# A linear-attention and expert kernel: VectorE makes attention's rows of batches 1 and 3 in front of a residual and of the router, and the scores' low half in front of w1's

## The reference

```python
x = x + attention(layernorm(x))      # q, k = elu(.)+1;  v
#   per row:  s += k v^T;  z += k;  out = (q s) / (q z + 1e-6);  out @ Wo + bo
x = x + moe(layernorm(x))
#   logits = x @ router_w^T;  two largest of 8, softmax over the two
#   y_e = gelu(x @ w1_e^T + b1_e) @ w2_e^T + b2_e;  sum of the two, weighted
```

## Time and profile before

| | us |
|---|---|
| median of 3 runs | 1016.1 (1013.57 to 1018.55) |
| profiled execution | 1024.98 |
| its span, first to last instruction | 1023.2 |

### The profile page before, as it was taken

The page is one execution under the profiler, slowest core; times in us unless marked ns, Lnnn a source line. Parts: engine busy times, 40 slices in busy tenths (PEclk is TensorE's granted clock), DMA queues, the critical chain, the costliest instruction groups (busy, mean ns, idle before and its releaser), DMA issues. The chain is left out here.

```text
span 1023.2 us, 33647 instructions
## 1 busy us (share of the span) xinstructions
PE 913.0 (89%) x10722; PEld 740.2 (72%) x10723; DVE 758.2 (74%) x2280; ACT 680.7 (67%) x1295; POOL 658.2 (64%) x580
## 2 busy tenths in 40 slices
PE   6788899899989998999987559899999999999994
PEld 3577677767766677766766338678999999999994
DVE  5788788888898888889887566456666666666673
ACT  7868888898888888898875414445555555555552
POOL 3245877788778877887773543347655665656565
PEclk9999899999999999999998779999999999999998
DMA  6726744554455354645451743435655556555554
GB/s 172 203 76 204 249 126 147 170 161 136 150 152 176 124 152 149 182 128 147 139 156 44 283 136 69 69 60 94 95 95 90 98 89 98 89 98 88 94 92 50
DMA packets 102583, 131.31 MB, mean 128 GB/s; under 512 B 15056, under 2 KB 89296, under 8 KB 101648
## 3 DMA queue, kind: packets, MB, share of 16 engines
q1 hardware_dynamic: 74336, 92.54, 32.4%
q0 software_dynamic: 25680, 35.01, 18.6%
q10 hardware_dynamic: 2464, 2.38, 0.7%
HBM read 64.29 MB, written 65.60 MB: 127 GB/s over the span
## 5 line engine op out<-in xcount | busy, mean ns | idle before, releaser
L1907 POOL DMA_INDIRECT out<-yt,to_token x135 | 216.6, 1604 | 176.2 <-DMA out<-yt,to_token 80.4
L1269 DVE SCALAR_TENSOR_TENSOR ahl<-pS,ahl 128x512 f16<-128x512 f32 x240 | 161.2, 682 | 42.1 <-ACT ahl L980 39.7
L980 ACT ACTIVATE ahl<-pS 128x512 f16<-128x512 f32 x240 | 142.2, 599 | 49.8 <-PE pS L652 36.0
L1783 POOL DMA_INDIRECT expert_in<-xn,cur x128 | 131.1, 1024 | 30.8 <-issue 26.0
L1191 ACT ACTIVATE g<-pS,b1s 128x256 f32<-128x256 f32 (+1 forms) x140 | 57.3, 462 | 94.1 <-PE pS L562 94.1
L562 PE MATMUL pS<-gT,w1s 128*128 128x256 f16 (+1 forms) x840 | 96.8, 271 | 4.0 <-DVE gT L1697 4.0
L562 PE MATMUL pF<-w2s,ghl 128*128 x816 | 95.3, 273 | 2.4 <-issue 1.6
L1704 DVE TENSOR_TENSOR ghl<-g,ghl 128x1024 f16<-128x1024 f32 (+1 forms) x68 | 83.0, 1221 | 18.8 <-ACT ghl L1216 12.5
L1777 POOL TENSOR_TENSOR state<-state,ut 128x272 f32<-128x272 f32 x64 | 49.9, 779 | 72.2 <-DVE ut L1309 71.3
L562 PE MATMUL pU<-w2s,ghl 128*128 x804 | 94.4, 273 | 1.6 <-issue 1.1
L562 PE MATMUL pF<-xT,was 128*128 128x512 f16 x384 | 92.8, 379 | 3.2 <-DVE xT L1274 3.0
(11 more groups left out here) (223 smaller groups left out, 2184.3 us busy)
## 6 DMA issues: line engine op xcount, KB each, us to landing
xg<-expert_in SPq DMA_DIRECT2D x64, 260.0 KB
qk_parts<-qkhl SPq DMA_DIRECT2D x64, 256.0 KB, 2.4
qst<-qk_parts SPq DMA_DIRECT2D x192, 64.0 KB
kst<-qk_parts SPq DMA_DIRECT2D x96, 128.0 KB
xs<-x SPq DMA_DIRECT2D x16, 512.0 KB
out<-x SPq DMA_DIRECT2D x16, 512.0 KB
w1raw<-w SPq DMA_DIRECT2D x16, 256.0 KB
w2raw<-w SPq DMA_DIRECT2D x4, 1024.0 KB, 7.0
```

Of the source, the lines that this page charges most:

```text
L980: nc.scalar.activation(ahl[:, b % 2, 0, n * 4 * C:(n + 1) * 4 * C], score_bank(fr, n)[:], ACT.Relu).then_inc(sc_hi, 1)
L1269: V.scalar_tensor_tensor(ahl[:, b % 2, 1, cols], score_bank(fr, n)[:], 0.0, ahl[:, b % 2, 0, cols], ALU.max, ALU.subtract).then_inc(sc_lo, 1)
L1783: G.indirect_dma_start(xg_dram, bass.IndirectOffsetOnAxis(ap=cur[:, qp, 2 * b + t:2 * b + t + 1], axis=0), xn2[:, qp, b], None).then_inc(s ...
L1907: G.indirect_dma_start(out, bass.IndirectOffsetOnAxis(ap=to_token[:, c % 2, s:s + 1], axis=0), yt[:, c % 2, s], None, compute_op=ALU.add). ...
```

## The change

VectorE's code: `router` is cut in two. `router_logits`, its first two instructions, stays where `router` was, and the rest comes behind `attention(3)`, `state_part(3)` and `logit_part(s, 2)`. `attention(1)` comes in front of `residual(s, 0)`, `score_lo(2, 3)` in front of `norm1_shift` and `w1_low`. On ScalarE `out_hi(s, 1)` and `score_hi(2, 2)` come in front of `norm2_apply(1)`. On TensorE the transposes of batch 1 wait for `x1_done` of batch 0 as well. No instruction is added or taken away.

```diff
--- before.py
+++ after.py
@@ -689,6 +689,8 @@
                     if g:
 
                         pe.wait_ge(lga_done, g)
+                        if b == 1:
+                            pe.wait_ge(x1_done, g)
                     for k in range(KC):
                         mm = nc.tensor.transpose(pA[:, k * C:(k + 1) * C], at[:, k * P:(k + 1) * P], ident)
                     mm.then_inc(aT_ps, 1)
@@ -1121,11 +1123,11 @@
                     score_hi(2, 1)
                 if fr and c >= 2:
                     w1_high()
+                if bk:
+                    out_hi(s, 1)
+                    score_hi(2, 2)
                 if normed:
                     norm2_apply(1)
-                if bk:
-                    out_hi(s, 1)
-                    score_hi(2, 2)
                 if normed:
                     norm2_apply(2)
                 if bk:
@@ -1357,7 +1359,7 @@
                     ins.then_inc(rt, 1)
                     dve.wait_ge(rt, RT * step + links[0])
 
-                def router():
+                def router_logits():
                     links[0] = 0
                     dve.wait_ge(lga_done, 4 * r + 4)
                     dve.wait_ge(ln2_rs, r + 1)
@@ -1368,6 +1370,8 @@
                     dve.wait_ge(lg_sum, r + 1)
                     link(r, V.scalar_tensor_tensor(lg[:], lga[:, rp], 1.0 / WS, rs2[:].unsqueeze(2).to_broadcast([P, B, E]),
                                                    ALU.mult, ALU.mult))
+
+                def router():
                     carry_wait(dve)
                     for b in range(B):
                         ins = V.max(mx[:, b], lg[:, b])
@@ -1516,6 +1520,7 @@
                 if ahead:
                     norm1_stats(i + 1, 0, 2)
                 if c == STEPS + 1:
+                    router_logits()
                     router()
                     for b in range(B):
                         norm2_apply(b)
@@ -1534,18 +1539,17 @@
                     norm2_shift()
                 if bk:
                     score_lo(2, 0)
+                    attention(1)
                     residual(s, 0)
-                    attention(1)
                     state_part(1)
                     score_lo(2, 1)
                     out_lo(s, 1)
                     score_lo(2, 2)
+                    score_lo(2, 3)
                 if ahead:
                     norm1_shift(i + 1)
                 if fr and c >= 2:
                     w1_low()
-                if bk:
-                    score_lo(2, 3)
                 if fr:
                     values(0)
                 if bk:
@@ -1563,11 +1567,13 @@
                 if c == STEPS + 1:
                     w2_low(0)
                 if ro and c != STEPS + 1:
-                    router()
+                    router_logits()
                 if bk:
                     attention(3)
                     state_part(3)
                     logit_part(s, 2)
+                if ro and c != STEPS + 1:
+                    router()
                 if c == 1 and not front:
                     w1_low()
 
```

More of the change, by code:

```diff
@@ L1123, in body @@
                     w1_high()
-                if normed:
-                    norm2_apply(1)
                 if bk:
@@ L1128, in body @@
                     score_hi(2, 2)
+                if normed:
+                    norm2_apply(1)
                 if normed:
```

## The result

| | before | after |
|---|---|---|
| median, us | 1017.33 (1013.57 to 1020.6, 4 runs) | 1025.89 (1024.0 to 1027.21, 4 runs) |
| profiled execution / its span | 1024.98 / 1023.2 | 1025.69 / 1023.9 |
| a step, median of c=4 to c=14 | 33.41 | 34.15 |
| start of step c=15 in the span | 502.88 | 511.05 |
| VectorE busy | 758.2 | 764.1 |

After is slower: the ratio is 1.0084, 95% interval [1.0044, 1.0124]. I had forecast 1006.8 with a range up to 1016.5. The steps are 0.74 us longer where I had them 0.71 shorter.

The account below looks back on a forecast made before the run. No engine was full; TensorE's handover waits cost 3.1 us a step, and VectorE bound the later part. 13 x (0.53 + 0.18) = 9.2 us, plus 0.1 from the ends, gave 9.3: 1006.8 us, own range 1002 to 1010.5, overall 1000 to 1016.5.

Parts of the forecast that it names:

- the margin: VectorE's `w1s` in its new place: starts 0.53 us ahead of GpSimd's `state`, so it keeps its 0.73 us.
- rival 2: `w1s` held up about 0.5 us by the scatter it starts in; 3.3 us gained in all, 1012.8; chance 0.14.
- Rival 3: `w1s` comes behind `state` if ScalarE's high part is over 0.53 late; 7.3 us lost, 1023.4; chance 0.10.
- place 1: Router's rest behind `attention(3)`: the first projection, and the second with it, start earlier, gaining 0.53 us a step.
- Place 2: `attention(1)` before `residual(0)`: transposes start earlier but scores (2,3) do not; worth nothing to TensorE.
- Place 3: `score_lo(2, 3)` before `norm1_shift` and `w1_low`: the 0.73 us wait at (3,1) goes, 0.18 reaches the step's end.
- The ends: End of the attention stage: +1.1 us at step c=16, -1.0 in the last step; 0.1 us gained in sum.
- The wait for the counts in the last step: TensorE's positions wait for counts from the router's moved rest; the transposes and what follows come 1.0 us later.
- The profile's own offset: The profiled execution before lies 8.9 us above the median of runs; the difference carried over as it is.

Follow-up runs that it names:

- e1: The changed kernel with GpSimd's scatter (1,1), and so `state` of batch 1, waiting until `w1s`'s low half is made; step 33.08 us, ratio 1.0003 to the kernel before.
- e3: The kernel before with only `score_lo(2, 3)` moved in front of `norm1_shift` and `w1_low`; step 34.49 us, ratio 1.0144 to the kernel before.
- e5: The changed kernel with GpSimd waiting for `w1s` only in front of `state` of batch 1; step 33.03 us, ratio 0.9986 to the kernel before.
- e9: The kernel before, unchanged, profiled and timed a second time; step 33.42 us, ratio 1.0006.
- e8: The changed kernel with `score_lo(2, 3)` back behind `norm1_shift` and `w1_low`; step 33.10 us, ratio 0.9949 to the kernel before.
- e6: The changed kernel with GpSimd doing `state` of batch 1 first, then waiting for `w1s`, then two scatters; step 33.03 us, ratio 0.9967 to the kernel before.
- e7: The changed kernel with `norm1_shift` back before `score_lo(2, 3)` and `w1_low` behind `score_lo(3, 1)`; step 32.97 us, ratio 0.9939 to the kernel before.
- e10: The changed kernel, unchanged, profiled and timed again; step 34.25 us, ratio 1.0113 to the kernel before.
- e11: e7 again, unchanged, on the other chip; step 32.99 us, 1019.94 us, ratio 0.9979 to the kernel before.
- e12: e11 with the whole router back in front of `attention(3)` in the last step only; step 33.09 us, 1015.95 us, ratio 0.9943 to the kernel before.
- e4: The changed kernel with `w1_low` moved behind `score_lo(3, 1)`, `norm1_shift` left in place; step 33.62 us, ratio 1.0038 to the kernel before.

## Why the prediction was wrong

**The step that failed** is "For `w1s` in the new place I take 0.73: it starts 0.53 ahead of `state`, since GpSimd, which waits for ScalarE earlier in the step, moves with the rest." GpSimd did move with the rest. But the margin counted only `w1s` and took what stands in front of it, `sh`, at its old length. Without the hold `w1s` would have started near 330.23, 0.42 ahead of `state`; `sh`, which I had moved along at its old 0.16, took 0.62 and used that up. The term measured +1.02 us a step against my nothing (e1 and e3 show it from both sides).

Nor would the margin have saved it. e5 shows that a `state` ready behind a scatter holds VectorE while the scatter still runs, and by e9's count it does so from 0.36 into the scatter on; the forecast had `w1s` 0.54 into it (327.21 against 326.67). The row that I couldn't explain, `w1s` at 1.27 at 526.61, fits: it started 0.39 into a scatter with `state` directly behind. I had it before me, and put it down to the scatter alone, as rival 2, at 0.14. And the trace of before had a tiny instruction held in every step, which I overlooked: the `sh` of the second normalisation, beside a GpSimd instruction with tensors in SBUF.

```profile
314.18 1.06 DVE L1287 SCALAR_TENSOR_TENSOR sh<-mv,rs 128x4 f32<-128x4 f32 x1
```

```profile
314.07 1.15 POOL L1770 TENSOR_TENSOR qkhl<-qf,qkhl 128x512 f16<-128x512 f32 x1 [0.21 <-ACT qkhl L1013]
```

Rival 3, `w1s` behind `state`, gave 1023.4, the nearest to 1025.9, but that is in part luck: I had it come about by a late ScalarE, at no cost for `sh`, and with 0.53 from place 1. The sentence of the Trainium skill (SBUF — State Buffer, Who interferes with whom) has the right engine pay for `w1s` here: `state` went first and kept 0.78. The price is a little under a full block: `w1s` was 0.61 longer than beside an idle GpSimd (1.29 against 0.68), when 0.73 of `state` were left. On an instruction held before the other has started, as `sh` is, the sentence says nothing; the runs show that.

**Place 1** was over-sized: 0.53 forecast, 0.17 to 0.21 measured. The first projection gains about what I said, 0.50 (2.94 into the step, before 3.44), with the 0.24 of waiting for `xT`. But behind it the output projection of batch 3, at 310.34, needs `x1` of batch 2: VectorE makes it at 309.78 + 0.41, behind the router's rest. I followed the first projection and took it that the second moves by the same; it starts 5.69 into the step, before 5.91.

**Place 2**: nothing forecast and nothing found up to the scores (2,3), with the `x1` wait of 0.48; 0.12 behind them, from a cause that I don't know (e8).

**Place 3's handovers** were right: no wait at (3,1), 0.52 at (2,3), and in e5 and e6, where nothing collides, 0.31 at (3,2). Of the 0.18 forecast for the end of the step 0.10 is there; e1, e5 and e7 stand 0.02 to 0.13 below e8.

**The ends**: 0.1 forecast, 0.15 by e9 and e10, and that the two agree is luck, since two profiles of one kernel lie 1.4 apart there. The wait for the counts in the last step came as forecast. Its price, 1.0 forecast, is 0.5 up to the router's end (e11, e12), and e12's time says more. The positions of step c=16 start 35.43 into the stretch from c=15 on in e10 and 37.21 in e9, 1.8 earlier where I had 1.1; this, too, is given back by the first expert product.

**The profile's own offset.** I carried over the 8.9 us by which the profiled execution lies above the median, unexplained. A part of it may be the outside waits of the last step, which the first profile of before has and five others have not. Against it: e9 has them as well and its profiled execution, 1021.13, lies below its median, 1022.71. Their price was not measured on one chip; the kernel before takes 1018.37 on the chip without them and 1021.88 and 1022.48 on the other. The offset changed no sign, but it made the two first profiles look alike (span 1023.2 and 1023.9) where the medians are 8.6 apart. e1 and e5, where nothing collides, gain 0.33 and 0.38 a step; 13 x 0.35 would have been near 4.5 us. The whole times of the kernels without the collisions scatter around that: e1 is 0.7 us longer than the kernel before on its chip, e5 2.2, e11 2.5, e6 4.1, e7 5.5 and e12 6.5 us shorter.

## What to carry to other kernels

When a two-SBUF-operand instruction of VectorE is moved, lay GpSimd's queue beside the new place and count the whole group that moves, the tiny ones as well: four numbers a row cost half a microsecond here. A GpSimd tensor instruction that is ready behind a running scatter can hold VectorE before it has started itself; here it did from 0.36 us into the scatter on, tested with `state` alone. Give such work a place where GpSimd is idle, as e7 does with `w1s`; that added no wait in front of the scores. And compare the ends of two profiles only if they are from one chip; and even then an end can differ by a microsecond or more (104.88 and 106.25 for one kernel). Repeated parts, such as these steps, tell 0.05 us where whole times tell 2 to 4.

## What the runs showed of the hardware

- `sh` (two operands, 128x4) takes 0.15 beside a scatter with nothing ready behind it (e5, 0.48 in) and 0.62 beside the same scatter with `state` behind it (after, 0.50 in); 0.65 in e4 and 0.75 in e3, where it starts 0.48 and 0.38 into the scatter. Each time it lasts to within 0.1 of the scatter's end. Started 0.16 into such a scatter, with `state` behind it, it takes 0.15 (e9, step c=3).
- `w1s` takes 0.68 with GpSimd idle (e7) and 1.29 if it starts 0.05 after `state` of 0.78. The scatter behind `state` is then longer as well, 1.25 instead of 0.99: it starts at 331.60 while `w1s` runs to 331.99. Beside `w2s` of 2.28 a scatter takes 3.08 instead of 0.96 (e11).
- Four loads of 1 MB take SyncE 4.1 us to issue on one chip and 9.3 to 10.9 on another, with waits of up to 7 us on VectorE for something outside the engines. What they wait for isn't in the records that I read; it is open.
